# A mixture of experts and an attention-MLP block on one core: the expert rows gathered straight from x, and the work around the expert loop moved ahead of it and into it

## The chip, the core and the metric

The kernel runs on one core of a Trainium2 chip. The time is device time in microseconds (us) of one execution. Engines: PE is TensorE (matrix products), PEld its weight load, ACT ScalarE, DVE VectorE, POOL GpSimd, SP the engine that issues most of the DMAs. Each runs its own program and waits for the others by semaphores.

## The reference

`x` holds 4 sequences of 512 rows of 512 values (2,048 rows in all).

```python
h = _layernorm(x)                       # eps 1e-5
expert = min(clip(token_id, 0, 24999) // 6250, 3)      # 4 experts, chosen by the token's id
# for each row, with the 512x512 matrix C[e] of its expert (Wg = Wu = Wd = C):
y = (silu(h @ C.T) * (h @ C.T)) @ C.T
x = x + tanh(g_xattn) * y

h = _layernorm(x)
a = _rmsnorm(h, ln1_w)                  # 16 heads of 32, causal softmax attention
mod = 0.1 * tanh((attention(a, Wq, Wk, Wv, Wo)) @ A)   # A is 512x16, B 16x2048
m = _rmsnorm(h, ln2_w)
gate = silu(m @ W_in.T + mod * (m @ A) @ B)
out = x + tanh(g_ffn) * (h + (gate * (m @ W_up.T)) @ W_down.T)
```

## The kernel before

All large products are made from values in two parts. ScalarE rounds a value to the product's format (the high part), VectorE or GpSimd subtracts it from the value (the low part), and TensorE adds high x high, low x high and high x low. So every operand of a product waits for a rounding and a subtraction.

**Indices.** VectorE makes a one-hot of each row's expert from the ids (line 1035), TensorE counts ranks with two products (lines 488 and 489, after six constants of GpSimd, lines 381 to 399), and VectorE turns the counts into the position of every row in an order sorted by expert (lines 1038 to 1048) and, later, into a table of items (lines 1103 to 1127). An item is 128 sorted rows with one expert; there are 16 + 3 = 19.

**Ahead of the items.** SP loads all of x in four tiles of 1 MB (line 212), then two experts' weights (line 218), and the other two when their staging is free (line 223). VectorE takes the statistics of the 16 tiles of 128 rows (line 1083), ScalarE normalises them (line 805), and GpSimd scatters each to `x_sorted` in HBM (line 404). ScalarE rounds the four experts' weights (line 799, by the helper of line 793), VectorE makes all four low parts (line 1095). When all 16 scatters have landed, SP loads item 0 (line 233).

**The item loop** (lines 540 to 544 on TensorE, with counterparts on the other engines): turn 128 rows (line 501), first product with the expert's weights (12 instructions of line 479), silu (823), gate (1138), turn (516), second product (12 more), copy of y (line 837, by 793), and SP stores it to `y_sorted` (line 240). Each engine works in program order. TensorE's order for item i is: first product of i, turn of i + 1, second product of i - 1, turn of the activation of i. The low parts are lines 1133 (x) and 1142 (activation).

**Between the loop and the batches.** `wov` is loaded within the loop; after it TensorE multiplies Wo with A (line 556) and Wv with the result (line 564). VectorE scales `wqk` by the norm's weights (lines 1159 and 1160). When every y is stored, GpSimd gathers the first 512 rows of it (line 434), VectorE adds them to x and takes statistics (1259, 1262), computes the factors (lines 1274 to 1301), ScalarE normalises (938), TensorE turns the rows (line 780), SP stores the residual (312), loads it back (319) and then loads the first two chunks of MLP weights (282, 285).

**The batches.** For each of the 4 sequences: projections of queries and keys (line 596), the low rank part (711), values (699), then heads: queries and keys are stacked by small DMAs (line 300), scores (611), softmax, values; then 16 chunks of the MLP, in which the next sequence's y is gathered, added and normalised between chunks. GpSimd also makes the low parts of the projection weights (line 438, operations of 128x1024) and scales a part of the probabilities (line 449, 128x256), beside VectorE's line 1198. Line 1227 is VectorE's low part of a weight chunk, two operands in SBUF; line 1280 is one of the small operations of the factors.

The wait that ties the start of the items to all else, and the one that starts the next stage (lines 242 to 244 and 428):

```python
            sp.wait_ge(items_ok, 1)
            sp.wait_ge(scattered, 16 * NT)
            load_item(0)
...
            pool.wait_ge(y_stored, 16 * ITEMS)
```

## Time and profile before

| | us |
|---|---|
| median of 3 runs (range) | 1156.31 (1155.48 to 1157.55) |
| the profiled execution | 1155.6 |
| its span, first to last instruction | 1153.6 |
| TensorE busy | 1053.0 (91%) |
| VectorE busy | 719.8 (62%) |
| ScalarE busy | 622.8 (54%) |
| GpSimd busy | 167.4 (15%) |

The profile is one execution. An engine's busy time counts its own instructions; an idle time is put down to the event that ended it. Positions are microseconds from the span's start. In the windows, the clock (PEclk) is what was granted to TensorE as a share of full speed, 2.4 GHz; at half of it the engine runs at 1.2 GHz.

### The profile page before, as it was taken

What the parts mean: (1) busy time and instruction counts of PE and PEld (TensorE: products, weight loads), DVE (VectorE), ACT (ScalarE), POOL (GpSimd) and SP (SyncE); (2) the same over time, 40 slices, a digit from 0 to 9 for tenths busy, and PEclk for the clock granted to TensorE, in tenths of its full rate; (3) what the DMA queues carried; (4) which work ended last, traced back from release to release, by engine and by line L of the source; (5) the groups of instructions that cost most, each with busy time, mean ns of one, the idle gap of its engine ahead of it and who ended that gap; (6) DMA issues with size and microseconds to landing.
All of it is one profiled execution on the core that took longest, in us unless ns stands there. A gap on an engine that the chain in (4) does not pass through costs nothing.

```text
span 1153.6 us, 18580 instructions
## 1 busy us (share of the span) xinstructions
PE 1053.0 (91%) x5384; PEld 885.5 (77%) x5385; DVE 719.8 (62%) x1591; ACT 622.8 (54%) x1466; POOL 167.4 (15%) x138
## 2 busy tenths in 40 slices
PE   0299995899999999998999999989999999899998
PEld 0178885688778888887788888877888888778887
DVE  7332326589766555898565558995564589944443
ACT  4233331588654444786544437885444378854442
POOL 4520002123300000333000013230000033200000
PEclk9999996799999999999999999999999999999999
DMA  7555231533333332523432326324332353323331
GB/s 276 189 141 163 92 109 56 169 69 82 120 110 93 98 118 84 137 55 100 138 99 82 121 65 167 68 65 163 93 98 82 100 157 81 73 73 92 93 98 45
DMA packets 52977, 124.44 MB, mean 108 GB/s; under 512 B 7441, under 2 KB 7441, under 8 KB 52369
## 3 DMA queue, kind: packets, MB, share of 16 engines
q1 hardware_dynamic: 50368, 115.55, 34.1%
q0 software_dynamic: 2560, 8.39, 2.1%
q14 instruction: 36, 0.29, 0.1%
q8 instruction: 13, 0.21, 0.1%
HBM read 80.92 MB, written 17.83 MB: 86 GB/s over the span
## 4 chain that ended last, share of the span: by engine, by line
PE 76%; DVE 11%; issue 5%; ACT 5%; DMA 2%; POOL 1%; DVEq 0%; ACTq 0%; SPq 0%; POOLq 0%
PE bank L479 60%; PE bank L629 5%; PE bank L642 4%; PE bank L611 3%; DVE wr L1177 3%; DVE nb L1189 3%; ACT big L881 2%; PE bank L671 1%; ACT wr L793 1%; DVE big L1198 1%; PE bank L613 1%; ACT big L805 1%; DVE wch L1227 1%; POOL x_sorted L404 1%; PE bank L501 1%
## 5 line engine op out<-in xcount | busy, mean ns | idle before, releaser
L479 PE MATMUL bank<-wr,wch 128*128 128x512 f32 x1536 | 373.2, 392 | 0.0
L479 PEld LDWEIGHTS bank<-wr,wch 128*128 128x128 f32 x1536 | 288.0, 188 | 64.0 <-issue 1.2
L479 PE MATMUL bank<-wch,actr 128*128 128x512 f32 x768 | 185.5, 391 | 3.6 <-DVE actr L1177 3.6
L479 PEld LDWEIGHTS bank<-wch,actr 128*128 128x128 f32 x768 | 143.4, 188 | 35.0 <-DVE actr L1177 5.3
L1227 DVE SCALAR_TENSOR_TENSOR wch<-stream,lns,wch 128x256 fp32r<-128x256 f32 x256 | 122.3, 539 | 50.9 <-ACT wch L920 50.9
L1177 DVE TENSOR_TENSOR wr<-bank,wr 128x512 fp32r<-128x512 f32 (+1 forms) x240 | 135.0, 608 | 29.2 <-ACT wr L793 28.8
L881 ACT ACTIVATE big<-bank,nb 128x512 f32<-128x512 f32 (+3 forms) x256 | 131.5, 531 | 15.9 <-DVE nb L1189 14.8
L793 ACT ACTIVATE wr<-bank 128x512 fp32r<-128x512 f32 (+1 forms) x240 | 111.3, 535 | 37.8 <-PE bank L479 22.8
L793 ACT ACTIVATE actr<-act_sb 128x512 fp32r<-128x512 f32 x64 | 40.4, 632 | 147.3 <-DVE act_sb L1240 147.3
L479 PE MATMUL bank<-wr,actr 128*128 x456 | 116.6, 406 | 3.3 <-DVE actr L1142 1.5
L1189 DVE TENSOR_REDUCE nb<-bank 128x1 f32<-128x512 f32 (+3 forms) x256 | 107.2, 479 | 6.5 <-PE bank L613 5.9
L449 POOL TENSOR_SCALAR big<-big,rr 128x256 f32<-128x256 f32 x64 | 77.9, 1217 | 218.3 <-DVE rr L1194 218.3
L920 ACT ACTIVATE wch<-stream,lns 128x256 fp32r<-128x256 f32 x256 | 108.4, 494 | 0.8 <-DMA stream<-in_wmlp 0.8
L438 POOL TENSOR_TENSOR wr<-wstage,wr 128x1024 fp32r<-128x1024 f32 x16 | 38.8, 2426 | 467.8 <-ACT wr L793 467.8
L479 PE MATMUL bank<-wr 128*128 128x512 f32 x384 | 101.9, 415 | 3.3 <-DVE wr L1177 2.8
L928 ACT ACTIVATE sil<-bank 128x512 f32<-128x512 f32 x64 | 38.1, 596 | 119.8 <-PE bank L671 119.7
L629 PE MATMUL bank<-ident,big 128*128 128x128 f32 x640 | 86.7, 278 | 17.0 <-DVE wr L1177 16.9
L479 PEld LDWEIGHTS bank<-wr,actr 128*128 128x128 f32 x456 | 84.5, 192 | 21.3 <-issue 4.4
L1177 DVE TENSOR_TENSOR wch<-stream,wch 128x512 fp32r<-128x512 f32 x64 | 44.2, 691 | 82.9 <-ACT wch L793 82.2
L629 PEld LDWEIGHTS bank<-ident,big 128*128 128x128 f32 x640 | 70.6, 140 | 30.3 <-DVE wr L1177 21.7
L642 PE MATMUL bank<-wr 128*128 128x512 f32 (+3 forms) x512 | 91.9, 321 | 0.0
L479 PEld LDWEIGHTS bank<-wr 128*128 128x128 f32 x384 | 74.0, 200 | 19.7 <-issue 3.1
(152 smaller groups left out, 1162.5 us busy)
## 6 DMA issues: line engine op xcount, KB each, us to landing
stream<-in_wmlp SPq DMA_DIRECT2D x64, 512.0 KB, 4.0
stack<-wr SPq DMA_DIRECT2D x192, 128.0 KB, 2.3
stream<-in_wmlp SPq DMA_DIRECT2D x64, 256.0 KB, 2.7
big<-in_x SPq DMA_DIRECT2D x8, 1024.0 KB, 7.9
xi<-x_sorted SPq DMA_DIRECT2D x19, 256.0 KB, 2.6
y_sorted<-ysb SPq DMA_DIRECT2D x19, 256.0 KB, 2.0
stream<-in_wexp SPq DMA_DIRECT2D x4, 1024.0 KB, 11.2
residual<-big SPq DMA_DIRECT2D x4, 1024.0 KB, 5.2
```

The costliest lines, as they stand in the source:

```text
L438: g.tensor_tensor(dst, src, high.bitcast(F32), ALU.subtract).then_inc(done, 1)
L449: g.tensor_scalar(rows, rows, rr[:, n % 2, qt:qt + 1], None, ALU.mult).then_inc(pn_pool, 1)
L479: mm = pe.matmul(dst, lhs(pl, k), rhs(pr, k), start=start and i == 0, stop=stop and i == n - 1, skip_group_check=skip)
L629: mm = pe.transpose(bank[bk][:, col + (qt - kt) * P:col + (qt - kt) * P + P], prob[par][:, src:src + P], ident[:, :])
L642: mm = pe.matmul(bank[ATT][:, kt * P:S], vst[:, kt, 64 * j:64 * j + P], pts[:, j % 2, part, at:at + w], start=False, stop=False, skip_grou ...
L793: return a.activation(dst, src, ACT.Copy)
L881: a.activation(prob[par][:, at:at + w], bank[bk][:, col:col + w], ACT.Exp, bias=nb[:, qt:qt + 1], accum_out=rs[:, par, qt:qt + 1]).then_in ...
L920: ins = a.activation(dst[:, :, dt, :], raw[:, :, dt, :], ACT.Copy, scale=lns[:, 1, dt:dt + 1])
L928: a.activation(sil[:, :], bank[GATE[par]][:, :], ACT.Silu).then_inc(g_silu, 1)
L1177: v.tensor_tensor(dst, src, high.bitcast(F32), ALU.subtract).then_inc(done, 1)
L1189: v.reduce_max(nb[:, qt:qt + 1], bank[bk][:, col:col + P * (qt + 1)], AXX, negate=True).then_inc(nb_ok, 1)
L1227: ins = v.scalar_tensor_tensor(out=dst[:, :, dt, :], in0=raw[:, :, dt, :], scalar=lns[:, 1, dt:dt + 1], in1=high[:, :, dt, :].bitcast(F32) ...
```

## The change

- **Rows.** x is no longer loaded, normalised and scattered ahead of the items. A second set of products on TensorE inverts the sorting, so that for each item there are the row numbers to gather (`gidx`), to scatter to (`sidx`) and the expert (`itab`). GpSimd gathers an item's rows straight from x into a ring of eight slots, VectorE takes their statistics and factors in groups of 1, 3, 3, 4, 4, 4 items, ScalarE normalises one item at a time. Items are ordered by sequence, so that the first sequence is covered by the first 7 items. GpSimd scatters every item's result to its own row in HBM, so that y is read back by plain loads.
- **Weights.** All four experts have staging of their own and are loaded at once. VectorE makes the low parts of experts 1 and 2, GpSimd those of 0 (while VectorE computes the indices) and of 3 (after four gathers; four more follow it).
- **The seam behind the loop.** Wo, Wv and A are multiplied ahead of the items; `wqk` is scaled by GpSimd between items 5 and 8; the low part of B is made partly by VectorE; the first sequence's y is added, normalised and turned during items 10 to 17; its residual is stored and reloaded, and the first two chunks of weights are loaded, during the loop.
- **Later sequences.** y of the next sequence comes by one DMA of SP in place of four gathers.

The core of the diff, by engine:

```diff
--- sync (SP): the loads
+            load_expert(0)
+            sp.dma_start(araw[:, :, :], amat).then_inc(a_in, 16)
+            sp.dma_start(wo_raw, wov[:, 0, :]).then_inc(wo_in, 16)
+            load_expert(1)
+            sp.dma_start(lns[:, :, :], ln).then_inc(small_in, 16)
+            sp.dma_start(gt[:, :], gates.broadcast_to([P, 2])).then_inc(small_in, 16)
+            load_expert(2)
+            sp.dma_start(wv_raw, wov[:, 1, :]).then_inc(wv_in, 16)
+            load_expert(3)
+            sp.dma_start(x1, x_tiles[0]).then_inc(x1_in, 16)
+
+            sp.wait_ge(exp_hi, E)
+            sp.wait_ge(exp_lo, E)
+            sp.dma_start(wstage[:, :, :], wqk).then_inc(wqk_in, 16)
...
+            def load_y(b):
+
+                rows = y_tiles[bass.ds(b, 1)]
+                sp.wait_ge(hb_turned, b * TT)
+                sp.dma_start(hb, rows).then_inc(y_in, 16)
...
                 if more:
+                    load_y(b + 1)
                     load_x(b + 1)
...
             sp.wait_ge(vw_mm, 2)
+            sp.wait_ge(y_stored, 16 * FIRST_ITEMS)
+            sp.dma_start(hb, y_tiles[0]).then_inc(y_in, 16)
+            sp.wait_ge(bst_ok, 3)
+            for c in range(2):
+                load_chunk(0, c, c, first=True)
             store_residual(0)
             sp.wait_ge(res_out, 16)
+            sp.wait_ge(xn_ok, 16)
             load_residual(0, first=True)
+            sp.wait_ge(y_stored, 16 * ITEMS)
             batch(0, True, first=True)
--- gpsimd
+            expert_low(0)
+            pool.wait_ge(oa_ok, 1)
+            g.tensor_tensor(inv_rhs[:, :, 1, :], oa[:, :, :], ewt[:, :].unsqueeze(2).to_broadcast([P, NT, IC]),
+                            ALU.mult).then_inc(wts_ok, 1)
+
+            def gather(i):
+                if i >= NS:
+
+                    pool.wait_ge(xn_ok, i - NS + 1)
+                elif RING[i] < 8:
+
+                    pool.wait_ge(vw_mm, 2)
+                g.indirect_dma_start(ring(i), None, x[0:T, :],
+                                     bass.IndirectOffsetOnAxis(ap=gidx[:, i:i + 1], axis=0)).then_inc(row_in[i % NS], 16)
+
+            def scatter(i):
+                pool.wait_ge(y_copied, i + 1)
+                g.indirect_dma_start(ys, bass.IndirectOffsetOnAxis(ap=sidx[:, i:i + 1], axis=0),
+                                     ysb[:, :], None).then_inc(y_stored, 16)
+
+            def turn(i):
+                for k in range(NS + 2 if i else NS, NS + 3):
+                    if i + k < ITEMS:
+                        gather(i + k)
+                scatter(i)
+
+            pool.wait_ge(index_ok, 1)
+            for i in range(4):
+                gather(i)
+            expert_low(3)
+            for i in range(4, NS):
+                gather(i)
...
             g.memset(braw, 0.0).then_inc(bst_ok, 1)
...
+            for k in range(4):
+                cols = slice(F // 4 * k, F // 4 * (k + 1))
+                g.tensor_copy(bst[:, cols], braw[:, cols]).then_inc(bst_hi, 1)
+                turn(k + 1)
+
+            pool.wait_ge(wqk_in, 16)
+            for dt in range(DT):
+                turn(5 + dt)
+                g.tensor_scalar(wqk_v[:, 0, dt, :], wqk_v[:, 0, dt, :], lns[:, 0, dt:dt + 1], SCALE, ALU.mult, ALU.mult)
+                ins = g.tensor_scalar(wqk_v[:, 1, dt, :], wqk_v[:, 1, dt, :], lns[:, 0, dt:dt + 1], None, ALU.mult)
+            ins.then_inc(wqk_ok, 1)
+            for i in range(5 + DT, ITEMS):
+                turn(i)
+                if i == ITEMS - 4:
+                    pool.wait_ge(wq_hi, 1)
+                    g.tensor_tensor(wqs[:, LO, :, :, :], wqk_v[:, :, :, 0:P], wqs[:, HI, :, :, :].bitcast(F32),
+                                    ALU.subtract).then_inc(wq_lo, 1)
--- tensor
-            pe.wait_ge(const_ok, 6)
+            pe.wait_ge(const_ok, 2)
             pe.wait_ge(onehot_ok, 1)
...
+            for t in range(NT):
+                pe.wait_ge(place_ok, t // (NT // OC_PARTS) + 1)
+                mm = pe.matmul(bank[0][:, 128:128 + 2 * IC], inv_lhs[:, t, :],
+                               inv_rhs[:, t, :, :].rearrange("p m i -> p (m i)"), start=t == 0, stop=t == NT - 1)
+            mm.then_inc(inv_ok, 1)
...
             def turn_x(i, first=False):
-                pe.wait_ge(xi_in, i * 16 + 16)
+                pe.wait_ge(xn_ok, i + 1)
...
+            for i in (last - 2, last - 1):
+                item_step(i)
+                if i == last - 2:
+
+                    pe.wait_ge(prep_ok, 1)
+                for dt in (0, 1) if i == last - 2 else (2, 3):
+                    turn_rows(0, (dt,), FIRST_ROWS)
--- scalar
+            expert_high(0)
+            expert_high(1)
+
+            act.wait_ge(bd_zero, 1)
+            act.wait_ge(woa_ok, 1)
...
+            expert_high(2)
+            expert_high(3)
+
+            def normalise_rows(i):
+                act.wait_ge(norm_ok, GROUP_OF[i] + 1)
+                if i:
+
+                    act.wait_ge(x_turned, i)
+                a.activation(xi[:, :], ring(i), ACT.Identity, bias=lmb[:, i:i + 1],
+                             scale=lma[:, i:i + 1]).then_inc(xn_ok, 1)
...
+            for i in range(1, ITEMS - 1):
+                silu(i)
+                x_high(i + 1)
+                if i + 2 < ITEMS:
+                    normalise_rows(i + 2)
+                if i == ITEMS - 2:
+                    rows_high(0, (0, 1), FIRST_ROWS)
+                copy_y(i - 1)
+                act_high(i)
+                if i == 2:
+                    values_high()
+                elif i == ITEMS - 6:
+                    act.wait_ge(wqk_ok, 1)
+                    split_wqk(0, 0)
+                elif i in (ITEMS - 5, ITEMS - 4):
+                    for j in (0, 1) if i == ITEMS - 5 else (2, 3):
+                        norm_rows(0, j)
--- vector
+            expert_low(1)
+            expert_low(2)
+            item_stats(0)
+            item_factors(0)
+            for i in GROUPS[1]:
+                item_stats(i)
+            x_low(0)
+            item_factors(1)
+            gated(0)
+            x_low(1)
...
+            for i in range(1, ITEMS - 1):
+                gated(i)
+                x_low(i + 1)
+                if i == 1:
+                    item_stats(6)
+                    item_factors(2)
...
+                elif i == 8:
+                    item_factors(4)
...
+                act_low(i)
+                if i == 3:
+                    values_low()
+                elif i in (6, 7):
+                    low_rank_low(i - 6)
...
```

The factors of a group (`item_factors`) are, on VectorE, a memset, one `bn_aggr` per item, and thirteen small operations on 128xn values, each waiting for the last. The index chain between the counts and `index_ok` is, each line waiting for those above it:

```python
# 128x64 or smaller, some in pairs: copy of the counts, scan, subtract, (subtract, add), (add, subtract),
# (shift, copy), (copy, shift), (subtract, copy), (scan, multiply-add), (subtract, compare 128x256),
# subtract, multiply 128x256, reduce 128x256, add, multiply 128x128, reduce 128x128, (subtract, compare 128x320)
v.tensor_tensor(inv_rhs[:, :, 0, :], oa[:, :, :], vt[:, :].unsqueeze(2).to_broadcast([P, NT, IC]), ALU.mult)
for k in range(OC_PARTS):       # 4 comparisons of 128x512
    v.tensor_tensor(inv_lhs[:, n * k:n * k + n, :], ..., ALU.is_equal).then_inc(place_ok, 1)
```

## Rows read from the trace of the kernel before

**Rows 1.** The page, part 2: TensorE's busy tenths in 40 slices

```profile
PE   0299995899999999998999999989999999899998
```

**Rows 2.** Windows by stage: stretch, its length, busy us (count) by engine, PEclk, DMA share, GB/s

```profile
0.00:49.94 49.94, 1.12 (x5) 0.98 (x6) 32.52 (x110) 20.29 (x22) 28.55 (x40) 1.00 0.72 264
49.94:180.30 130.36, 126.19 (x611) 103.03 (x611) 40.89 (x65) 42.28 (x77) 6.51 (x2) 1.00 0.39 116
...
180.30:209.30 29.00, 14.20 (x80) 13.54 (x79) 19.05 (x54) 8.09 (x14) 6.92 (x5) 0.57 0.25 82
...
223.90:1153.60 929.70, 898.30 (x4636) 756.98 (x4636) 621.43 (x1354) 544.20 (x1340) 123.03 (x90) 1.00 0.34 97
```

**Rows 3.** Chain of waits ahead of the first item: start us, us, what

```profile
43.19 2.72 DMA x_sorted<-big,pos
```

**Rows 4.** Timeline of the first 6 us: start us, us, engine, line, operation [idle before, releaser]

```profile
3.08 0.28 DVE L1035 TENSOR_TENSOR oh<-ge 128x64 f32<-128x64 f32 x1
...
4.58 0.69 PE L488 MATMUL bank<-oh,tri 128*128 128x64 f32 x2 [4.58 <-POOL maskr L399]
...
5.73 0.29 DVE L1038 COPY cnt<-bank 128x128 f32<-128x128 f32 x1 [2.37 <-PE bank L489]
```

**Rows 5.** Groups by line and shape, first 240 us: xcount, busy us, mean ns, idle before

```profile
L805 ACT ACTIVATE big<-big,lnb,lna 128x512 f32<-128x512 f32 x16 | 11.5, 799 | 6.0 <-DVE lna L1091 6.0
...
L1083 DVE BATCH_NORM_STATS2 st<-big 128x6 f32<-128x512 f32 x16 | 9.7, 678 | 0.0
...
L793 ACT ACTIVATE wr<-stream 128x2048 fp32r<-128x2048 f32 x4 | 7.5, 1901 | 4.4 <-DMA stream<-in_wexp 4.4
...
L1069 DVE TENSOR_TENSOR nr<-nr 128x8 f32<-128x8 f32 x9 | 1.5, 167 | 0.3
```

**Rows 6.** Line 212, the four loads of x (1 MB each): time to landing

```profile
DMA to landing us min/median/max: 5.4/8.3/11.1
```

**Rows 7.** Timeline of one item's steps

```profile
67.01 3.02 PE L479 MATMUL bank<-wr,actr 128*128 x12
...
67.69 4.61 POOL L423 TENSOR_TENSOR bst<-big,bst 32x2048 fp32r<-32x2048 f32 x1
67.98 0.69 DVE L1142 TENSOR_TENSOR actr<-bank,actr 128x512 fp32r<-128x512 f32 x1 [2.70 <-ACT actr L793]
...
70.22 3.00 PE L479 MATMUL bank<-wr,actr 128*128 x12
```

**Rows 8.** Timeline from batch 0's first product to its first scores

```profile
209.29 8.45 PE L479 MATMUL bank<-wr 128*128 128x512 f32 x24 [2.75 <-DVE wr L1177]
...
218.42 0.69 DVE L1177 TENSOR_TENSOR wr<-bank,wr 128x512 fp32r<-128x512 f32 x1 [2.31 <-ACT wr L793]
...
219.41 2.39 POOL L438 TENSOR_TENSOR wr<-wstage,wr 128x1024 fp32r<-128x1024 f32 x1 [22.18 <-ACT wr L793]
...
223.85 0.50 PE L611 MATMUL bank<-stack 96*128 96x512 f32 x1 [1.42 <-DVE xi L1319]
...
224.99 4.56 PE L479 MATMUL bank<-wr 128*128 128x512 f32 x12
```

**Rows 9.** Line 1227 from 219 to 223, and line 1280: ns min/median/max

```profile
L1227 DVE SCALAR_TENSOR_TENSOR wch<-stream,lns,wch x4: 474/476/2671, 219.0 to 222.4; 128x256 fp32r<-128x256 f32 x4
...
L1280 DVE TENSOR_SCALAR nr<-mv x4: 170/170/1046, 196.2 to 840.0; 128x4 f32<-128x4 f32 x4
```

**Rows 10.** Timeline around the last scatters

```profile
39.77 2.29 DVE L1095 TENSOR_TENSOR wr<-stream,wr 128x2048 fp32r<-128x2048 f32 x1 [1.92 <-ACT wr L793]
40.25 2.64 POOL L404 DMA_INDIRECT x_sorted<-big,pos  x1 [0.30 <-issue]
...
43.19 0.96 POOL L404 DMA_INDIRECT x_sorted<-big,pos  x1 [0.30 <-issue]
```

**Rows 11.** Line 449, GpSimd's scaling of probabilities: ns min/median/max

```profile
L449 POOL TENSOR_SCALAR big<-big,rr x64: 1126/1227/1234, 228.0 to 1007.8; 128x256 f32<-128x256 f32 x64
```

**Rows 12.** DMA issues, first 240 us: gathers of y, us to landing

```profile
big<-y_sorted,pos POOLq DMA_INDIRECT x4, 3.8
```

605 lines of the change are left out of this document (305 added, 300 removed).

## The prediction

> **What bounds the kernel now.** I read the page's slices first, then the windows by stage, then the chain of waits, and last the timeline around each seam. The slices show TensorE at nine tenths or more nearly everywhere except in the first slice or two and around slice 7 [rows 1]. The windows put numbers on it: TensorE works 1.1 us in the first 49.9, then 126.2 of 130.4 us in the loop over the 19 expert items, then 14.2 of 29.0 us, and 898.3 of the last 929.7 us in the four batches [rows 2]. The batches are TensorE's own time, and the change leaves their code almost as it is. So the gain has to come from the two seams: 49.9 us before the first item, and 43.6 us from the end of the item loop (180.3) to the first scores (223.85).
>
> The chain says why the seams are long. Ahead of the items all 2,048 rows are normalised and scattered to HBM; the last scatter leaves at 43.19 and lands 2.72 us later [rows 3], then the first item's rows are read back, and TensorE starts at 49.94. Behind the loop nothing of the next stage is ready: the last result is stored, `wov` is multiplied, results are gathered, normalised, turned, and the chain ends with the residual's store and, behind it, the first chunk of weights.
>
> **The change, part by part.**
>
> *(a) Indices.* Before, TensorE counted ranks at 4.58, when GpSimd's sixth constant was ready, and VectorE took the counts 1.15 us later; the one-hot had been ready at 3.36 [rows 4]. Now the product needs two constants and the one-hot, so the counts come at about 3.4 + 1.2 = 4.6. The new chain is longer. A dependent small operation lasts 0.17 us [rows 5] and starts some 0.03 after the last; wider ones (64 to 256 elements, often in pairs) I take at 0.25 to 0.45. Twelve levels from the counts end at 8.5.
>
> There the first piece of GpSimd's new work begins. Expert 0 lands like the first tile of x, 5.4 us after an issue at about 1.2 [rows 6], and ScalarE rounds it in 1.90 [rows 5]: 8.5. GpSimd's low part of 128x2048 costs 4.61, by the row with as many elements per partition [rows 7] (the 128x1024 one, 2.39, doubled gives 4.8 [rows 8]): it ends at 13.1. What do VectorE's small operations do meanwhile? In the trace a VectorE operation with two SBUF operands took 2671 ns instead of 474 when GpSimd's 2.39 us subtraction ran from 219.41 to 221.80, and a tiny 128x4 operation took 1046 instead of 170 behind another [rows 8, 9]. So I take the chain as stopped from 8.5 to 13.1. By the Trainium skill, SBUF — State Buffer (Who interferes with whom), the pair of ports is an exclusive lock held for the whole instruction, whoever starts first. By that rule size does not matter and the chain stops as costed; the trace agrees.
>
> From 13.1: some seven small levels (1.8), GpSimd's product of 320 elements, which needs the same operands (0.8), four comparisons of 128x512 at 0.6 to 0.7 (2.6), the last four products and the read of the bank (0.8) give the row indices at 19.1 and the item table at 19.6.
>
> *(b) To the first item.* Of the 16 scatters none is left ahead of the items; four gathers are. One costs 0.96 alone plus 0.30 of issue, but 2.64 where VectorE's subtraction of 128x2048 (39.77 to 42.06) overlaps it: it ended 0.83 us after that one did [rows 10]. All four scatters over 1.5 us lie so. VectorE makes the low parts of experts 1 and 2 in 2.29 each [rows 10], 19.6 to 24.1. So the gathers end at 20.3, 22.7, 24.9 and 26.2. By the Trainium skill, the same page and section, descriptor generation is held up only by a VectorE operation in a 2-port mode, not by a `tensor_tensor` (it marks this as inferred); the gathers would then end at 24.1, and with all else the sum would be 2 us smaller. The row differs, and the row decides.
>
> Then comes the piece the change is named after: GpSimd's low part of expert 3, 26.5 to 31.1. Its weights are no limit: before, the fourth tile of x (1 MB each), issued at 4.5, landed 11.1 us later, three tiles in 9 us behind the first [rows 6]; expert 3 is now the sixth such load: 6.6 + 5 x 3.0 = 21.6, rounded at 23.5. Beside it VectorE has item 0's statistics (0.68 [rows 5]) from 24.1 and sixteen small operations for the factors: half are done at 26.5, the rest are stopped until 31.1 and end at 32.4. ScalarE normalises in 0.80 [rows 5]; the first turn starts at **33.3** instead of 49.9: 16.6 us gained. Made by VectorE this piece would take 2.3 instead of 4.6, and the same count gives about 31.0; alone it costs some 2 us.
>
> *(c) The item loop.* Its period before is 6.41 us, TensorE-bound (its two products start at 67.01 and 70.22, the next item's at 73.42: the rows show half a period, 3.21 [rows 7]). What is new per item: on ScalarE 0.80 for normalising, in a gap of 2.4 us ahead of the copy of y; at single items 1.1 to 1.6 more, in a gap of 2.0. On VectorE up to 1.4 of statistics or 3.2 of factors between the low parts of x and of the activation, a gap of 2.7; what exceeds it meets a slack of 1.5, as the activation's low part ended at 68.67 and was needed at 70.22 [rows 7]. VectorE's three fixed steps read PSUM and were not stretched beside GpSimd's 4.61 us subtraction (67.69 to 72.30) [rows 7]. GpSimd's queue: a gather, a scatter, 2 x 1.26, against 6.41. At items 5 to 8 it also scales `wqk`, two operations of 128x512. The nearest row, 128x256, is 1.23 [rows 11]; it starts together with VectorE's scaling, so part of it may be waiting. Bounds: the row itself, and twice it, 2.4. I take 1.2; 2.5 + 2.4 = 4.9 fits. At 2.4 the queue falls back 0.9 us an item, 3.6 in four, and catches up after. A scatter must have landed before the next copy of y: 1.26 and 3.8 of landing, the longest row of an indirect transfer [rows 12], within the 6.4 from copy to copy. So I cost the loop at 130.3, plus 16 turns of the residual rows at 0.09 apart (1.5), plus 2.0 for collisions (the first items' factors behind GpSimd's memsets, the factors at item 8 behind `wqk`): bounds 0 and 8. The end of the last product: 33.3 + 130.3 + 1.5 + 2.0 = 167.1.
>
> *(d) The seam behind it.* `wov`'s products move ahead of the items, where TensorE is idle until 33.3; without that cover they would cost what they did before, some 11 of the 14.2 us of this window [rows 2]. Adding y, norms, turns, the residual's store and reload, and the chunks' loads all move into the loop. Behind the last product come 24 products (2 x 2.9 at the loop's 0.24 each, 12 from 67.01 to 69.9, instead of 8.45 [rows 7, 8]), low rank 8 x 0.24 = 1.9, values 24 x 0.13 = 3.1: TensorE is done at +10.8. The second projection is split at +7.3, and from there the scores took 4.73 before (low part done 219.11, scores 223.85: the stack's transfers, and VectorE's 2671 ns row) [rows 8, 9]; nothing in that stretch changes, GpSimd's subtraction included. So scores at +12.0 instead of 43.6: 31.6 gained. The last scatter lands at about +5 and is covered. The next projection, 4.56 at the low pace [rows 8], should take 3.0: 1.5 more. In the idle seam the granted clock was 0.57 of full speed, in the loop 1.00 [rows 2].
>
> *(e) The batches.* The 4 gathers of y per batch on GpSimd become one 1 MB transfer on SP ahead of x's. It waits for nothing new (the turns it waits for are a batch old), and stands on SP's queue between the last stack load and x. Behind it the next chunks come 1 MB later, 3.0 us [rows 6]. Cost 0, since TensorE, busy 898.3 of 929.7 us there [rows 2], has two whole chunks in hand then; without that cover 3 us for each of three batches.
>
> **The sum.** 16.6 - 1.5 - 2.0 + 31.6 + 1.5 = 46.2. The profiled execution took 1155.6 (span 1153.6): 1109.4. The median of the three runs, 1156.31, is 0.7 above it: 1110.
>
> **Rivals.**
>
> *A, the small operations are not stopped.* The stretched rows have 128x256 and 128x4 operands; none is a two-input operation of 64 elements. Then indices come at 14.8, GpSimd's last low part starts when expert 3 is rounded (23.5), and the first turn is at 28.2: 5.1 us better, 1105. Against it: the 1046 ns row [rows 9].
>
> *B, the loop is stretched.* If a copy of y waits for the previous scatter each time (0.6 copy, 2.9 for a scatter at its longest, 3.8 landing) the period is 7.3, and 19 items cost 17 us more: 1127; with it only in the `wqk` stretch or at the blocked factors, 1115 to 1120. For it: GpSimd's queue holds many things in order. Against: VectorE has few two-input SBUF operations there.
>
> *C, slower than before.* The mechanism is GpSimd's queue as the loop's bound: gather and scatter each 2.94, landing 3.8 and the copy 0.6 in series make 10.3 us per item, 19 x 3.9 = 74 more: 1184. It decides above 6.41 + 46.2/19 = 8.8 us per item. Against it: gathers have eight slots of lead, so they need not stand in that series.
>
> **How the numbers follow.** The main case has 0.66 (own range 1105 to 1116: the spread of (a) and (b), and 0 to 8 in (c)), A 0.14, B 0.17, C 0.03, a third of this near its turning point. The range 1101 to 1124 takes in A and most of B. A difference of 0.2% is about what this kernel's measurement can tell from none: faster 0.97, same 0.01, slower 0.02.
>
> **What would show it.** Right: the first turn at 31 to 36; a stretched small VectorE operation beside each of GpSimd's two 4.6 us subtractions; second and third gather over 1.5 us; the item period 6.4; scores some 12 us behind the last product; the stretch from there to the end as long as before, 930. Wrong: the first turn at 28 (A); waits of ScalarE's copy of y for scatters, a period over 7 (B, C); or TensorE waiting in the batches for y or a chunk.

## The result and the profile after

The changed kernel takes **1117.39 us** (median of 4 runs, 1116.64 to 1118.48) against 1155.89 us for the kernel before in the same comparison (1154.34 to 1157.55): a ratio of 0.9667, 95% interval 0.9651 to 0.9684. That is 38.5 us faster where 46 was forecast; 1117.4 lies in the range 1101 to 1124, and 1.4 us above the main case's own range.

The slices of the page and the windows by stage after the change, to be laid beside [rows 1] and [rows 2] (columns as there):

```profile
PE   6499998999999999989999999999999999899998
...
0.00:38.46 38.46, 18.57 (x84) 18.18 (x86) 28.34 (x65) 10.69 (x11) 23.39 (x28) 1.00 0.63 231
38.46:173.67 135.21, 129.52 (x625) 105.63 (x626) 82.61 (x215) 62.24 (x107) 51.09 (x53) 0.99 0.33 115
173.67:185.22 11.55, 10.11 (x57) 8.67 (x56) 7.04 (x10) 8.56 (x16) 3.39 (x2) 1.00 0.32 81
185.22:1116.70 931.48, 898.23 (x4636) 757.05 (x4636) 621.45 (x1354) 544.47 (x1340) 111.56 (x78) 1.00 0.34 97
```

The dip at slice 7 has gone. By stage, before and after:

| stretch | before | after | gained | forecast |
|---|---|---|---|---|
| start to the first turn of an item | 49.94 | 38.46 | 11.5 | 16.6 |
| first turn to the end of the last product | 130.3 | 135.2 | -4.9 | -3.5 |
| last product to the first scores | 43.6 | 11.55 | 32.05 | 31.6 |
| first scores to the end | 929.75 | 931.5 | -1.7 | +1.5 |
| span | 1153.6 | 1116.7 | 36.9 | 46.2 |

So the seam behind the items came out half a microsecond better, and 9.7 us are missing in the other three rows, 5.1 of them ahead of the first turn.

**Ahead of the first turn.** The timeline (start us, us, engine, line, operation, [idle before, releaser]):

```profile
8.02 4.52 POOL L408 TENSOR_TENSOR wr<-stream,wr 128x2048 fp32r<-128x2048 f32 x1 [3.83 <-ACT wr L847]
8.15 4.42 DVE L1146 TENSOR_TENSOR shift<-sums,kf 128x16 f32<-128x16 f32 x1
...
16.88 2.49 DVE L1168 TENSOR_TENSOR hT<-iof,rct 128x512 fp32r<-128x512 f32 x4
...
17.70 3.57 PE L544 MATMUL bank<-hT 128*128 128x40 f32 x16 [1.75 <-DVE hT L1168]
...
21.31 0.24 DVE L1173 TENSOR_SCALAR gidx<-bank,iof 128x20 int32<-128x20 f32 x1 [1.95 <-PE bank L544]
...
21.83 2.27 DVE L1209 TENSOR_TENSOR wr<-stream,wr 128x2048 fp32r<-128x2048 f32 x1
21.85 5.51 POOL L423 DMA_INDIRECT big<-in_x,gidx  x1 [5.24 <-DVE gidx L1173]
24.03 2.27 DVE L1209 TENSOR_TENSOR wr<-wstage,wr 128x2048 fp32r<-128x2048 f32 x1
27.66 0.96 POOL L423 DMA_INDIRECT big<-in_x,gidx  x1 [0.30 <-issue]
...
29.82 0.69 DVE L1215 BATCH_NORM_STATS2 sti<-big 128x6 f32<-128x512 f32 x1 [3.52 <-DMA big<-in_x,gidx]
...
31.15 4.50 POOL L408 TENSOR_TENSOR wr<-wstage,wr 128x2048 fp32r<-128x2048 f32 x1
...
31.39 4.28 DVE L1232 TENSOR_TENSOR nm<-nm 128x1 f32<-128x1 f32 x1
...
38.46 1.09 PE L568 MATMUL bank<-ident,xi 128*128 128x128 f32 x4 [10.29 <-ACT xi L873]
```

GpSimd's low part of expert 0 stops one operation of 16 elements, which costs 0.17 alone, for 4.42 us: the chain stands from 8.15 to 12.57. The indices are ready at 21.3. The first gather starts in the same moment as two subtractions of VectorE, one right behind the other, and ends 1.06 us after both, 5.51 instead of 0.96. The last of the first four ends at 31.12, and only then does GpSimd begin the low part of expert 3; VectorE has by then reached item 0's factors, and a two-input operation on one value per partition takes 4.28 us. The one just before it, with one input (line 1230, 128x1), starts at 31.20, 0.05 us behind GpSimd's subtraction, and takes 0.15: it was not stopped. In the six profiles that have this place it is so each time (0.05 to 0.15 us behind the start, 0.15 long).

**In the loop.** The period of an item is 6.41 us as before (turns of activations at 57.81, 64.22, 70.62). The 4.9 us lie at four places; the turns of activations, laid beside those of the kernel before, give their sizes. The first, of 1.45, is at the first silu. Item 1's factors are stopped by GpSimd's memset (2.14 instead of 0.17) and ScalarE has still to load its table, so that the silu comes 9.55 us behind the first turn instead of 8.1:

```profile
41.17 2.14 DVE L1225 TENSOR_SCALAR nm<-mvi 128x3 f32<-128x3 f32 x1
...
41.46 1.82 POOL L447 MEMSET stream<- 96x2048 f32 x1
...
46.71 1.28 ACT L886 ACT_TABLE_LOAD   x1
```

The second, of 1.2, follows from it. TensorE idles longer before the next twelve products (2.4 us in all since the item's first product, 1.1 before the change), and they take 4.50 us where the same group took 3.02 before; the granted clock over them is 0.64 (last line; its columns as in [rows 2]), and it was 1.00 over that group before (0.3 of the 1.5 us is offset by a wait that TensorE had there before):

```profile
50.26 4.50 PE L517 MATMUL bank<-wr,actr 128*128 x12 [0.22 <-issue]
...
50.26:54.76 4.50, 4.50 (x14) 3.56 (x15) 1.45 (x3) 0.42 (x1) 0.76 (x1) 0.64 0.18 59
```

The third is one hiccup of 0.5 at 112 us: a scatter issued at 103.73, behind 1 MB of y and 1.5 MB of weights that SP had issued from 100.12 on, needs 7.4 us to land, and ScalarE's copy waits for it. The waits of that stretch (engine, line, releaser: us, times, longest) and the scatters' landing:

```profile
ACT ysb L847 <- DMA y_rows<-ysb,sidx: 3.3, 1, 3.3
...
DMA to landing us min/median/max: 2.7/2.7/7.4
```

The fourth is the turns of the first sequence's rows, forecast at 1.5: eight at 154.86 and eight at 162.15, each eight lengthening its item by 0.88 us. At 156 VectorE's residual rows (two operations in 3.29 us) meet GpSimd's subtraction of `wqk` (2.40), but TensorE's next turn comes 2.84 us behind the start of the products there, as in every item: this costs nothing.

**The seam and the batches.** The timeline around the first scores, and the same group of products a batch later:

```profile
173.49 5.60 PE L517 MATMUL bank<-hT,wqs 128*128 128x512 f32 x24
...
185.22 0.50 PE L669 MATMUL bank<-stack 96*128 96x512 f32 x1 [1.44 <-DVE xi L1407]
...
186.36 4.54 PE L517 MATMUL bank<-hT,wqs 128*128 128x512 f32 x12
...
422.74 2.96 PE L517 MATMUL bank<-hT,wqs 128*128 128x512 f32 x12
```

Twelve products take 4.54 us in batches 0 and 2, and 2.96 in batches 1 and 3; before it was 4.56, 4.55, 3.00, 2.96. The granted clock over the 4.54 us is 0.62, over the 2.96 us it is 1.00. The 1.5 us forecast from a warm seam are thus missing. Besides, each of the first three batches, taken from first scores to first scores, is some 0.6 us longer than before once the 1.5 of such a group is set aside (236.4 against 235.8 in batch 0, with the group of 4.5 in both; 234.9 against 235.8 in batch 1 and 236.2 against 234.1 in batch 2, with it in one of the two).

### The profile page after: what moved, and what is told of

It is laid out like the page before. It is cut to its first block, busy times and chain, and to the rows that moved or that the text cites. A ratio compares the mean times of both kernels' runs of the same rounds, so it can differ in the third digit from the quotient of the medians.

```text
span 1116.7 us, 18206 instructions
## 1 busy us (share of the span) xinstructions
PE 1056.4 (95%) x5400; PEld 889.5 (80%) x5401; DVE 739.4 (66%) x1643; ACT 626.0 (56%) x1473; POOL 189.4 (17%) x160
## 4 chain that ended last, share of the span: by engine, by line
PE 78%; DVE 10%; issue 4%; ACT 4%; DMA 2%; SPq 0%; DVEq 0%; POOL 0%; ACTq 0%; POOLq 0%
PE bank L517 61%; PE bank L687 5%; PE bank L700 5%; PE bank L669 3%; DVE wr L1268 2%; DVE nb L1280 2%; ACT big L925 2%; PE bank L729 1%; DVE big L1289 1%; PE bank L671 1%; ACT wr L847 1%; DVE wr L1318 1%; DMA stack<-wr 1%; DMA big<-in_x,gidx 1%; PE bank L568 1%
## 5 line engine op out<-in xcount | busy, mean ns | idle before, releaser
L517 PE MATMUL bank<-hT,wr 128*128 128x512 f32 x1536 | 373.2, 392 | 0.0
L517 PEld LDWEIGHTS bank<-hT,wr 128*128 128x128 f32 x1536 | 288.0, 188 | 64.0 <-issue 1.2
L517 PE MATMUL bank<-wr,actr 128*128 128x512 f32 (+1 forms) x1224 | 303.6, 398 | 7.1 <-DVE actr L1268 3.6
L517 PEld LDWEIGHTS bank<-wr,actr 128*128 128x128 f32 x1224 | 229.0, 190 | 56.9 <-DVE actr L1268 5.3
L1318 DVE SCALAR_TENSOR_TENSOR wr<-stream,lns,wr 128x256 fp32r<-128x256 f32 x256 | 122.3, 540 | 50.8 <-ACT wr L964 50.8
L964 ACT ACTIVATE wr<-stream,lns 128x256 fp32r<-128x256 f32 x256 | 108.4, 495 | 0.0
L517 PE MATMUL bank<-hT,wqs 128*128 128x512 f32 x384 | 98.9, 406 | 0.5
L1268 DVE TENSOR_TENSOR wr<-stream,wr 128x512 fp32r<-128x512 f32 x64 | 44.2, 691 | 82.9 <-ACT wr L847 82.2
L669 PE MATMUL bank<-stack 96*128 96x512 f32 (+3 forms) x256 | 78.1, 368 | 10.2 <-DVE xi L1407 5.5
L517 PEld LDWEIGHTS bank<-hT,wqs 128*128 128x128 f32 x384 | 72.1, 195 | 15.7 <-DVE wr L1268 1.7
```

What stands on the lines that cost most here:

```text
L517: mm = pe.matmul(dst, lhs(pl, k), rhs(pr, k), start=start and i == 0, stop=stop and i == n - 1, skip_group_check=skip)
L669: pe.matmul(bank[bk][:, col:col + w], stack[:, par, 0, qt * P:qt * P + P], stack[:, par, 1, 0:w], start=True, stop=False, skip_group_check ...
L964: ins = a.activation(dst[:, :, dt, :], raw[:, :, dt, :], ACT.Copy, scale=lns[:, 1, dt:dt + 1])
L1268: v.tensor_tensor(dst, src, high.bitcast(F32), ALU.subtract).then_inc(done, 1)
L1318: ins = v.scalar_tensor_tensor(out=dst[:, :, dt, :], in0=raw[:, :, dt, :], scalar=lns[:, 1, dt:dt + 1], in1=high[:, :, dt, :].bitcast(F32) ...
```

## The experiments

They ran on three occasions, each with runs of the kernel before beside them (medians 1153.47, 1153.74 and 1154.16); the ratios are taken within an occasion. Differences of 2 us in a median say little here: each execution has four groups of twelve products that take 3.0 or 4.5 us each, and the table's last column counts those of 4.5 in the profiled execution. So each kernel is also read by its first scores (us in the profile), ahead of which none of these four groups lies. The first twelve products behind the first turn of an activation, in the loop, do the same, though: in six of the twelve profiles (changed, changed again, low 0 on VectorE, `wqk` late, chunks spread, unused buffer) they take 4.5 to 5.3 us at a granted clock of 0.54 to 0.64, in the other six 3.0 us at 1.00. In the first six TensorE had idled 2.2 to 3.1 us in all between the item's first product and this group, in the other six 0.9 to 2.0. So an experiment that shortens this idle time can gain 1.5 us more at its first scores than it saves; that the shorter idle time is the reason was not tested by itself.

| kernel | median us (lowest to highest) | ratio, interval | first turn | first silu | first scores | groups of 4.5 |
|---|---|---|---|---|---|---|
| changed | 1117.39 (1116.64 to 1118.48) | 0.9667, .9651 to .9684 | 38.46 | 48.01 | 185.22 | 2 |
| changed again | 1118.31 (1115.36 to 1118.58) | 0.9679, .9655 to .9703 | 38.49 | 48.03 | 185.32 | 2 |
| low 3 on VectorE | 1116.45 (1114.69 to 1118.46) | 0.9667, .9645 to .9688 | 41.88 | 49.58 | 185.38 | 1 |
| statistics first | 1114.92 (1114.43 to 1117.81) | 0.9667, .964 to .9693 | 38.61 | 47.06 | 182.82 | 0 |
| low 0 on VectorE | 1117.39 (1116.78 to 1119.98) | 0.9679, .966 to .9699 | 39.09 | 48.62 | 187.02 | 2 |
| memsets early | 1115.08 (1112.85 to 1116.93) | 0.9663, .9641 to .9684 | 38.17 | 45.69 | 181.17 | 1 |
| low 3 on VectorE, `wqk` late | 1114.96 (1113.21 to 1116.29) | 0.9654, .9627 to .9682 | 36.40 | 45.72 | 183.05 | 2 |
| chunks spread | 1117.93 (1114.62 to 1119.34) | 0.9689, .9663 to .9715 | 38.17 | 47.71 | 184.50 | 0 |
| combined | 1107.24 (1104.5 to 1109.53) | 0.9593, .9568 to .9619 | 29.96 | 41.25 | 176.48 | 2 |
| unused buffer | 1117.12 (1112.47 to 1117.51) | 0.9664, .9634 to .9694 | 38.41 | 48.17 | 186.24 | 1 |
| combined, buffer last | 1107.47 (1106.97 to 1108.54) | 0.9593, .9575 to .9611 | 30.09 | 40.52 | 176.03 | 1 |

**Low part of expert 3 made by VectorE.** The part that the change is named after, undone.

```diff
 --- gpsimd
-            expert_low(3)
             for i in range(4, NS):
                 gather(i)
 --- vector
             expert_low(2)
+            expert_low(3)
             item_stats(0)
```

> The changed kernel with expert 3's low part made by VectorE, right behind those of experts 1 and 2, and not by GpSimd. Theory L (a VectorE operation with two SBUF operands and a GpSimd operation exclude each other for the whole instruction, and a gather that is caught by back-to-back subtractions waits for all of them): the first gather now waits for three subtractions, lasts about 7.8 us instead of 5.5 and ends near 29.6; its rows are there at 32.1, the factors are no longer stopped for 4.3 us, and the first turn starts at about 36.5 instead of 38.5: 2 us faster than the changed kernel. Rival F (the first gather is long by itself, a cost of the first indirect transfer): it still ends at 27.4, the first turn starts at about 33.2: 5 us faster.

The timeline, and the window 32 to 38 of this kernel and, second, of the changed one (columns as in [rows 2]):

```profile
21.96 7.71 POOL L423 DMA_INDIRECT big<-in_x,gidx  x1 [5.24 <-DVE gidx L1172]
24.14 4.47 DVE L1208 TENSOR_TENSOR wr<-wstage,wr 128x2048 fp32r<-128x2048 f32 x2
28.70 0.34 SPq L266 DMA_DIRECT2D wstage<-in_wqk  x1
...
37.35 0.69 DVE L1214 BATCH_NORM_STATS2 sti<-big 128x6 f32<-128x512 f32 x1 [8.73 <-DMA big<-in_x,gidx]
...
32.00:38.00 6.00, 0.00 (x0) 0.00 (x0) 0.65 (x1) 0.00 (x0) 4.48 (x6) 1.00 0.98 406
```

```profile
32.00:38.00 6.00, 0.00 (x0) 0.00 (x0) 5.69 (x12) 0.50 (x1) 5.54 (x3) 1.00 0.41 92
```

The gather is caught by three subtractions now and takes 7.71, ending 1.06 us behind the third: the hold grows with what VectorE has in a row. But the first turn came at 41.88, 3.4 us later instead of earlier, since the rows landed 7.7 us behind the end of their issue instead of 2.5. In that time the DMA engines were full (0.98, 406 GB/s) with the 2 MB of `wqk`, whose load waits for the last low part and was released at 28.70 rather than 35.73. At the first scores the two kernels are equal all the same (185.38 and 185.22): 1.85 us come back because item 1's factors no longer meet the memset, which leaves the silu 7.70 us behind the first turn instead of 9.55, and 1.5 because the twelve products behind it then take 3.03 us at a granted clock of 1.00 instead of 4.50.

**Item 0's statistics ahead of the subtractions.**

```diff
+            item_stats(0)
             expert_low(1)
             expert_low(2)
-            item_stats(0)
             item_factors(0)
```

> The changed kernel with VectorE's statistics of item 0 put ahead of the low parts of experts 1 and 2, so that VectorE reads no second SBUF operand while the gathers are issued. Theory L: the first gather takes 1.0 to 1.3 us instead of 5.5, its rows are there at about 25.3; the statistics end at 26; but the low parts on VectorE and GpSimd's of expert 3 now exclude each other (2 x 2.3 and 4.5 us one after the other), so the first turn starts at 37 to 40: within 2 us of the changed kernel. Rival F: the first gather still takes about 5.5 us, the statistics end at 30.5, the lows at 37 or later, the first turn starts at 42 or later: 3 us or more slower.

```profile
21.88 1.17 POOL L423 DMA_INDIRECT big<-in_x,gidx  x1 [5.24 <-DVE gidx L1173]
...
25.54 0.70 DVE L1215 BATCH_NORM_STATS2 sti<-big 128x6 f32<-128x512 f32 x1 [3.61 <-DMA big<-in_x,gidx]
...
26.15 2.28 DVE L1209 TENSOR_TENSOR wr<-stream,wr 128x2048 fp32r<-128x2048 f32 x1
26.82 5.95 POOL L408 TENSOR_TENSOR wr<-wstage,wr 128x2048 fp32r<-128x2048 f32 x1
28.34 6.58 DVE L1209 TENSOR_TENSOR wr<-wstage,wr 128x2048 fp32r<-128x2048 f32 x1
```

With VectorE waiting for the rows, the first gather costs 1.17 and the statistics come at 25.54, 4.3 earlier. The time is lost again at once: GpSimd's subtraction and VectorE's second one now stop each other (5.95 and 6.58 instead of 4.50 and 2.27), and the factors stand behind both. GpSimd's subtraction, which had waited behind VectorE's first, here got in ahead of VectorE's second, which no gather did. The first turn stays at 38.6. The first scores come 2.4 us earlier, which the low parts do not explain: the silu follows its turn by 8.45 us instead of 9.55, since the memset stops item 1's factors for less (0.97 instead of 2.14), and the twelve products behind it take 3.03 us instead of 4.50. That the first gather takes 1.17 here refutes rival F.

**Low part of expert 0 made by VectorE.**

```diff
 --- gpsimd
-            expert_low(0)
             pool.wait_ge(oa_ok, 1)
 --- vector
+            expert_low(0)
             expert_low(1)
```

> The changed kernel with expert 0's low part made by VectorE behind the index chain (ahead of experts 1 and 2), and not by GpSimd during it. Theory L: the operation at line 1146 takes 0.2 us instead of 4.42, the row numbers are there at about 17 instead of 21.5; the subtractions run to about 24.1 (three), the first gather ends near 25, GpSimd's low part of expert 3 runs from about 29 to 33.3, the first turn starts at about 36: 2 us faster. Rival G (the 4.42 us belong to that place in the chain, not to GpSimd's subtraction): the line still takes over 4 us, the rows come at 21, VectorE has 2.3 us more to do before the statistics: 2 us slower.

```profile
9.29 7.01 PE L533 MATMUL bank<-araw,big 128*128 128x16 f32 x32 [4.27 <-DMA big<-in_wov]
16.14 3.58 PE L543 MATMUL bank<-hT 128*128 128x40 f32 x16
...
20.29 7.71 POOL L422 DMA_INDIRECT big<-in_x,gidx  x1 [7.95 <-DVE gidx L1172]
```

The stopped operation takes 0.17 now (line 1145 here), so the hold was GpSimd's doing. But the indices gain 1.6 us and not 4.3: TensorE is in the 32 products of `Wo` and A until about 16.2, and its sixteen index products start there without any wait. The third subtraction then takes the rest back by holding the gather for 7.71. The first turn is at 39.09, where 36 was expected.

**GpSimd's memsets ahead of the indices.**

```diff
             expert_low(0)
+            g.memset(apad[:, :, :].bitcast(F32), 0.0).then_inc(pool_own, 1)
+            g.memset(zst[:, :].bitcast(F32), 0.0).then_inc(zst_zero, 1)
+            pool.wait_ge(exp_lo, 1)
+            g.memset(braw, 0.0).then_inc(bst_ok, 1)
             pool.wait_ge(oa_ok, 1)
...
-            g.memset(apad[:, :, :].bitcast(F32), 0.0).then_inc(pool_own, 1)
-            g.memset(zst[:, :].bitcast(F32), 0.0).then_inc(zst_zero, 1)
-            pool.wait_ge(exp_hi, E)
-            pool.wait_ge(exp_lo, E)
-            g.memset(braw, 0.0).then_inc(bst_ok, 1)
```

> The changed kernel with GpSimd's three memsets (2.9 us in all) moved from behind the eight gathers to the time when it waits for the index chain. They write SBUF and read none. 
```profile
8.47 4.37 DVE L1150 TENSOR_TENSOR dshift<-shift 128x16 f32<-128x16 f32 x1
...
40.89 0.17 DVE L1224 TENSOR_SCALAR nm<-mvi 128x3 f32<-128x3 f32 x1
...
45.69 0.60 ACT L885 ACTIVATE sil<-bank 128x512 f32<-128x512 f32 x1
```

The factors of items 1 to 3 run at 0.17 again, and the silu follows the first turn by 7.52 instead of 9.55. With the first turn 0.3 earlier, the first scores come at 181.17: 4.05 us gained. The turn and the silu account for 2.3 of them, and 1.5 more lie in the twelve products behind the silu, 3.03 us at a granted clock of 1.00 instead of 4.50 at 0.64.

**Low part of expert 3 on VectorE, and `wqk`'s load held until two items are turned.** It repeats the first experiment without the 2 MB beside the gathers.

```diff
             sp.wait_ge(exp_lo, E)
+            sp.wait_ge(x_turned, 2)
             sp.dma_start(wstage[:, :, :], wqk).then_inc(wqk_in, 16)
```

> e1 (expert 3's low part on VectorE) with the 2 MB load of wqk held back until two items' rows have been turned. In e1 the first gather's rows came 7.7 us after GpSimd had issued it (29.67 to 37.35), where the changed kernel's took 2.5, and e1 issues wqk's load at 28.70. Theory D (a gather that shares the DMA engines with a load of megabytes lands late): the rows are there 2.5 us after the first gather ends, at about 32.2, and the first turn starts at about 36.5, 2 us ahead of the changed kernel. Rival Q (the rows come late because seven more gathers stand right behind the first one): they still take 7 us or more and the first turn starts at 41 or later.

```profile
21.79 7.71 POOL L424 DMA_INDIRECT big<-in_x,gidx  x1 [5.24 <-DVE gidx L1173]
...
31.93 0.69 DVE L1215 BATCH_NORM_STATS2 sti<-big 128x6 f32<-128x512 f32 x1 [3.49 <-DMA big<-in_x,gidx]
...
36.40 1.09 PE L568 MATMUL bank<-ident,xi 128*128 128x128 f32 x4 [8.29 <-ACT xi L873]
```

The gather is held as long as in the first experiment, its rows land 2.4 us behind it again, and the first turn is at 36.40. So it was the load of `wqk` that made them late there, and not the seven gathers behind the first one, which stand there in both (rival Q). Against the changed kernel 2.06 us are gained at the first turn, 2.17 at the first scores.

**The first chunks' loads spread over four items,** instead of 1.5 MB at once.

```diff
             sp.wait_ge(bst_ok, 3)
-            for c in range(2):
-                load_chunk(0, c, c, first=True)
+            for k in range(4):
+                c, at, to, landed = k // 2, (0, CW)[k % 2], (CW, CW + D)[k % 2], (cg_in, cd_in)[k % 2]
+                sp.wait_ge(y_stored, 16 * (FIRST_ITEMS + 1 + k))
+                sp.dma_start(stream[:, c, at:to], wmlp[:, c:c + 1, at:to]).then_inc(landed[c], 16)
```

> The changed kernel with the four loads of the first two chunks (1.5 MB) issued one after each of four later scatters has landed, and not all at once behind the 1 MB of y. Theory D: the one scatter in 19 that lands 7.4 us after its issue (all others 2.7) is one that shares the DMA engines with these 2.5 MB; it lands in under 5 us, ScalarE's one wait of 3.3 us for it falls below 1, and TensorE gets 0.5 us back: 0.5 us faster. Rival W (GpSimd's scaling of wqk delays it): the 7.4 us and the 3.3 us stay.

```profile
DMA to landing us min/median/max: 2.7/2.7/3.5
```

The longest landing of a scatter falls from 7.4 to 3.5, ScalarE's wait for one is gone from the list of waits, and the first scores come 0.7 earlier, 0.3 of it already at the first turn. The cause of the hiccup is shown; its worth is under what the medians can tell.

**Combined.** The memsets early, `wqk`'s load held and the chunks' loads spread, as above, and the first gather kept clear of subtractions: VectorE waits for a flag that GpSimd sets behind the first gather, and all low parts but expert 0's are VectorE's.

```diff
 --- gpsimd
-            for i in range(4):
-                gather(i)
-            expert_low(3)
-            for i in range(4, NS):
+            gather(0)
+            g.memset(flag[:, :], 0.0).then_inc(g0_ok, 1)
+            for i in range(1, NS):
                 gather(i)
...
-                if i == ITEMS - 4:
+                if i == ITEMS - 3:
                     pool.wait_ge(wq_hi, 1)
 --- tensor: the first turn ahead of the waits for the weights
+            turn_x(0, first=True)
             pe.wait_ge(exp_hi, E)
             pe.wait_ge(exp_lo, E)
-            turn_x(0, first=True)
 --- scalar: the table loaded ahead of the first silu
             x_high(0)
+            act.wait_ge(const_ok, 5)
+            a.activation(warm[:, :], ones[:, 0:1], ACT.Silu).then_inc(act_own, 1)
 --- vector
+            dve.wait_ge(g0_ok, 1)
             expert_low(1)
-            expert_low(2)
             item_stats(0)
             item_factors(0)
+            expert_low(2)
+            x_low(0)
+            expert_low(3)
             for i in GROUPS[1]:
                 item_stats(i)
-            x_low(0)
```

> The parts together: VectorE starts its low parts only when GpSimd has issued the first gather; low parts of experts 1, 2 and 3 on VectorE, with item 0's statistics and factors between the first two and item 0's low part of x ahead of the third; TensorE turns item 0's rows before it waits for the weights; the memsets early as in e4; silu's table loaded ahead of its first use; wqk late as in e5; chunks spread as in e6; GpSimd's low part of wqk one item later, where VectorE has no operation with two SBUF operands. By theories L and D: first gather 1.2 us, first turn at about 30, first product at about 34.8 instead of 41.05, first silu at about 40.5 instead of 48.0, about 1.4 us less in the loop; 9 us faster than the changed kernel: 1108. If L is wrong about what waits for what, the first product starts at 38 or later and the gain is under 5 us.

```profile
21.80 1.18 POOL L432 DMA_INDIRECT big<-in_x,gidx  x1 [5.24 <-DVE gidx L1178]
23.14 2.29 DVE L1214 TENSOR_TENSOR wr<-stream,wr 128x2048 fp32r<-128x2048 f32 x1 [1.29 <-POOL flag L448]
23.28 2.97 POOL L432 DMA_INDIRECT big<-in_x,gidx  x1 [0.18 <-issue]
...
29.96 1.09 PE L571 MATMUL bank<-ident,xi 128*128 128x128 f32 x4 [1.83 <-ACT xi L876]
...
32.32 2.29 DVE L1214 TENSOR_TENSOR wr<-wstage,wr 128x2048 fp32r<-128x2048 f32 x1
...
35.73 5.48 PE L520 MATMUL bank<-wr,actr 128*128 x12 [4.68 <-issue]
```

This is the fastest kernel of the study: **1107.24 us**, 10 us under the changed kernel. The first turn is at 29.96, 8.5 us earlier, and the first scores 8.7 us earlier, but the one does not follow from the other. The first product comes 5.8 us behind the turn (the last line), since it waits for expert 3's low part, which ends only at 34.6 (for the 1.1 us between the profile names nothing); it is 5.3 us earlier than in the changed kernel (35.73 for 41.05). The rest comes behind it: 1.45 us from the earlier silu, 1.5 from the twelve products behind the silu (3.02 us instead of 4.50, granted clock 1.00 instead of 0.64), and 0.5 from the hiccup. The next bound is this low part.

**The changed kernel again.**

> The changed kernel itself, unaltered, on the same chip as the runs beside it: 1115 to 1119. Its trace should again show line 1146 at over 4 us and the first gather at 5.5. Of the four groups of 12 products that follow the first scores of a batch, 4.5 us in two and 3.0 in two of the changed kernel's trace, another number may come out slow: 1.6 us of span each.

The table has its stages: all within 0.1 us of the first profile, the stopped operation of line 1146 included (4.46), and the groups of 4.5 us again in batches 0 and 2. The times of the front end are no accident of one execution.

**An unused buffer of 4 bytes, and the combined kernel with its flag placed last.** The combined kernel had an unplanned gain behind its first scores: its feed-forward chunks followed each other in 8.41 us, where all kernels up to then had 8.46.

```diff
         warm = sb("warm", [P, 1])
+        flag = sb("flag", [P, 1])
```

> The changed kernel with a buffer of 4 bytes per partition that nothing uses, behind the one-column buffer that the table loads write; every buffer named after it lies 4 bytes further on. In the combined kernel the chunks of the feed-forward ran at a period of 8.41 us, in the changed kernel, its repeat and all the other experiments at 8.46. Theory P (the places of the buffers set that): the period is 8.41 here too, some 3 us are gained over four batches behind the first scores, and the median is 1114 to 1115. Theory N (it is another part of the combined kernel, such as the hold on the weights' load): the period stays 8.46 and the median is that of the changed kernel, 1117 to 1118. Up to its first scores the kernel stands as the changed one, at 185.2.

> The combined kernel with its buffer of 4 bytes behind all others, so that no other buffer is moved. Theory P: the chunks are back at a period of 8.46 us and the part behind the first scores is some 3 us longer, median 1110 to 1111; theory N: 8.41 and 1107 as before. In both the first turn stands at 30 us and the first scores at 176.5, which is the worth of the reordered front end by itself: 8.7 us against the changed kernel.

One chunk in the changed kernel, then in the one with the unused buffer:

```profile
349.09 2.94 PE L517 MATMUL bank<-hT,wr 128*128 128x512 f32 x12
...
357.31 0.40 PE L729 MATMUL bank<-zst,bchunk 96*128 96x512 f32 x1
```

```profile
348.23 2.89 PE L518 MATMUL bank<-hT,wr 128*128 128x512 f32 x12
...
356.40 0.39 PE L730 MATMUL bank<-zst,bchunk 96*128 96x512 f32 x1
```

The period is 8.41 with the buffer in between and 8.46 with it last: where the buffers lie sets it. What it brings, 0.05 us a chunk and 0.8 a batch (234.1 against 234.9), is real in the timeline and too small for the medians: both stayed where they were, which was the other theory's number. With the unused buffer the first scores came 1.0 us later, which was not expected. Of this 0.7 lies in one turn (1.12 us instead of 0.66) and the twelve products behind the first silu (5.19 instead of 4.50), over which the granted clock was 0.55 instead of 0.64; whether the buffer has to do with it is open. The gain of the combined kernel is its front end: placed last, its buffer leaves the first scores at 176.03 and the median at 1107.47.

## Why the prediction was right, and where its terms were off

The time lies in the stated range because that range is wide; the main case's own (1105 to 1116) missed it by 1.4 us. It also lies where rival B put its milder forms (1115 to 1120), but not for rival B's reason: ScalarE's copy waited for a scatter once, for 0.5 us of TensorE's time. The mechanism is the main case's, with terms that were too small, nearly all on the same side.

**What bounds the kernel.** Right: the gain is in the two seams, and TensorE's 898 us in the batches did not change (898.3 and 898.23).

**(a) Indices: 21.3 instead of 19.1.** The stop is right in place and length (8.15 to 12.57 for 8.5 to 13.1). The counts came at 5.27 instead of 4.6. The term mis-sized is "the last four products and the read of the bank (0.8)": the sixteen products of TensorE take 3.57 us in a row, longer than the comparisons they follow, and end 1.9 us behind the last of these. The third experiment adds that even without the stop TensorE's earlier products would have kept the index products until about 16.2. I had called TensorE idle until 33.3 and moved `wov`'s products there at no cost; of the 4.3 us that the freed chain could give they left 1.6.

**(b) To the first item: this is the step that failed.** I had the first gather unhindered at 20.3 and each following one getting in between two subtractions. [Rows 10] showed one subtraction alone. In the trace the gather got no opening between two that follow each other: 5.51 beside two, 7.71 beside three, 1.17 beside none. The statistics, forecast at 24.1, came at 29.82, and GpSimd's low part of expert 3 at 31.15 instead of 26.5; that is 2.2 from the indices and 2.4 from the gathers, nearly all of the 5.1 us by which the first turn was late. The rows' 2.5 us of landing, which in my sum lay beside the subtractions, came on top once the gather outlasted them.

The Trainium skill, SBUF — State Buffer (Who interferes with whom), infers that a `tensor_tensor` does not hold up descriptor generation. The experiments speak against it: only the subtractions beside the gather were changed, and it took 1.17, 5.51 and 7.71 us.

That VectorE's small operations are stopped whatever their size was right both times: 16 elements for 4.42 us, one element for 4.28. Both of these have two inputs. For all small operations the statement is too wide: one with a single input and a single element took its usual 0.15 beside the same subtraction (line 1230). Rival A, which denied it, is refuted; the undone part (line 1145: 0.17) shows GpSimd as the cause.

"Made by VectorE this piece alone costs some 2 us" was right by itself and wrong as a change: undone alone, the first turn came 3.4 us later, since the end of the last low part also releases a 2 MB load on SP's queue. With that load held back the first turn gained 2.06 us. I had counted the instruction and not what its semaphore sets free.

**(c) The loop: 4.9 instead of 3.5.** The period is 6.41 as forecast, and `wqk` scaled on GpSimd (0.71 to 1.73 an operation, 1.2 taken) held nobody up. The turns of the rows took 1.8 instead of 1.5. The term for collisions, 2.0, measured 3.1. It named the right place (factors behind the memsets), where the silu was 1.45 us later than before, behind its turn; it had no term for the clock behind it, 1.2 us, though the prediction had read the lower clock of an idle stretch from [rows 2]; and the hiccup took 0.5. "A scatter's 3.8 of landing, the longest row" was too short a bound: beside 2.5 MB of loads it was 7.4. Rival B was seen once, for 0.5 us, not as a period. Rival C is refuted.

**(d) The seam: 32.05 instead of 31.6.** Right. The next projection was forecast at 3.0 and took 4.54, with a granted clock of 0.62 over it (0.63 before), though TensorE was busy for 10.1 of the 11.55 us ahead of the scores. A seam of 29 us with TensorE half idle is thus not needed for the lower clock; the wait of 1.4 us for the stack lies right ahead of it in both kernels, but ahead of groups of 3.0 us too. What decides between them is open.

**(e) The batches: 1.7 us lost instead of nothing.** y's load cost no wait for a chunk. The 0.6 us a batch show as a wait of 0.71 us for a load of the stack at the end of the quads, absent at the same place before; what makes that load late is open.

## What to carry over

Before a piece of work is moved to another engine, list what its completion releases, the large loads on other queues above all: here undoing the move was worth 2 us at the first turn by the count of instructions, and lost 3.4 there until the load behind it was held. When a wait of TensorE is shortened, read the products behind it too: here 1.5 us of what several experiments gained lay in the clock granted to them. A gather issued by GpSimd wants a stretch in which VectorE has no run of two-input operations; give it one by a wait for a flag set behind the gather, and place long GpSimd subtractions and memsets where VectorE has no dependent chain of tiny operations. Of the 10 us that the combined kernel gained 8.7 stand ahead of its first scores, and came from such placing and the clock that followed it; it computes what the changed one computes.

## What the runs showed of the hardware that was not expected

- An indirect transfer beside bulk loads lands late far beyond its own size: 256 KB of rows after 7.7 us instead of 2.5 beside 2 MB, a scatter after 7.4 instead of 2.7. At the 406 GB/s of that window the 2 MB take 5.2 us (an estimate), as much as the rows were late; so they seem to have stood behind most of it. The Trainium skill, DMA: Bandwidth & Descriptors (Queues, rings and completion order), has each DMA engine take turns between queues packet by packet, by which I would expect a small transfer to be delayed less than that; the number here differs.
- A memset on GpSimd, which only writes, stopped a `tensor_scalar` of three elements on VectorE for 2 us (2.14 instead of 0.17, and 0.17 again when the memset was elsewhere). In the first experiment the same memset (1.82 us from 39.35) ran beside two-input operations of one value, and they took their usual 0.16 to 0.19. I had expected only two-input operations to be stopped; by the Trainium skill, SBUF — State Buffer (Who interferes with whom), a `tensor_scalar` can take the shared pair too, and the trace agrees.
- Twelve products behind the same short wait take 3.0 or 4.5 us, now one and now the other in batches 0 to 2 and always 3.0 in batch 3; the kernels of this study had none to two of the longer kind. The granted clock over a long one is 0.62 (186.36 to 190.90), over a short one 1.00. At 1.5 us each, a kernel's executions can differ by some 3 us by this alone. In the loop the same happens to the twelve products behind the first silu, there only in the profiles in which TensorE had idled longest.
- A gather that waits behind one of two subtractions of VectorE that follow each other does not get in between them; a subtraction of GpSimd did in the second experiment, and VectorE's second one, begun at 28.34, then took 6.58 us.
- Four bytes between two buffers changed twelve products from 2.94 to 2.89 us, by a cause that stays open.
